# A graph and mixture-of-experts layer on one core: the last expert's rows scattered by slot, the second bias moved ahead of the first expert

## The chip, the cores and the metric

The kernel runs on one core of a Trainium2 chip. The metric is device time in microseconds (us) of one execution; lower is better. A core has TensorE (PE), VectorE (DVE), ScalarE (ACT), GpSimd (POOL) and SyncE (SP), each with its own instruction stream, and 16 DMA engines that all of them share. Semaphores order the streams.

## What is computed

The input is 625 rows of 768 numbers and 10,000 edges. After a two-layer graph convolution and an attention block, the part that matters here is a feed-forward layer with eight experts. Each row chooses one expert by the largest gate logit:

```python
w, sel = jax.lax.top_k(gate_logits, K)          # K = 1
w = jax.nn.softmax(w, axis=-1)
combine = jnp.zeros((n, E)).at[jnp.arange(n)[:, None], sel].add(w)
hid = jax.nn.relu(jnp.einsum('nd,edf->enf', h2, W1) + b1[:, None, :])
y = jnp.einsum('enf,efd->end', hid, W2) + b2[:, None, :]
moe = jnp.einsum('ne,end->nd', combine, y)
return x + moe.reshape(b, t, d)
```

W1 is 8 x 768 x 3072, W2 is 8 x 3072 x 768. So a result row is `base` (everything else that is added up) plus the row's weight times (its expert's y plus that expert's bias b2).

## The kernel before

**Rows, slots and chunks.** Rows are held as 5 groups (c = 0 to 4) of 125 on the partitions. Each expert has 128 slots. The routing gives each row a slot, `own` = 128 times its expert plus its rank there; `home` is the same unless an expert has more than 128 rows, when the surplus goes to extra tiles that run only if they are needed (in this profile they don't: the page shows 128 weight loads, 16 for each of 8 experts). GpSimd scatters the normalised rows `n2` by slot into DRAM (`hs_d`, L548) and later reads one expert's tile at a time back (`next_in`, L554). The first expert's tile is not waited for: TensorE makes it with products of one-hot marks `oh0` and `n2` (L1639).

**One expert.** An expert is 16 chunks of 1152 KB: 8 of W1, 8 of W2. SyncE loads a chunk into one of four `raw` buffers (L442, L445), ScalarE makes its high part `whi` (`split_hi`, L599), VectorE its low part `wlo` (`split_lo`, L894), which frees the raw buffer for the load four chunks later. TensorE multiplies three pairs of high and low parts: 18 products for a W1 chunk (L1675) and 18 for a W2 chunk (L1694). Between them the hidden tile is read (`hid`), turned (L1662), biased (`bia`, L1258) and split (`hTT`). The result y of an expert is in banks 4 and 5 of PSUM; for experts 0 to 6 it is read into `ysb` and stored by slot into `ys_d` (`y_out`, L559). `tile(0)` is written out for the first expert with a few things of its own; the other seven run in hardware loops on each engine.

**The end.** While the last expert runs, GpSimd gathers for each row its y from `ys_d` into `x2` (`y_back`, L563, five indirect DMAs); rows of the last expert get zeros. VectorE adds `wtok` times that to `base` (L1279). The last expert's y doesn't go through DRAM: ScalarE and VectorE split it, and TensorE spreads it back to the rows with products by turned marks `oh7T` (`spread_y`, L1715), on top of products of b2 with the turned choice `oh8T` (`bias_y`, L1710). VectorE adds `wtok` times the sum to `base` for each group (L1289), and SyncE stores the group (L456, two DMAs each).

**What sets the order.** Each engine's order is written out by hand. Around the change it is:

- TensorE ahead of the first expert: ranks (L1619, L1622), 50 filling products of a matrix of ones (`keep_busy`, L1330, whose results nobody reads), the first tile (L1639), 24 more filling products, then the first expert. In `tile(0)`, after chunk 1, `marks_turned` turns the marks of the last expert (L1648) and the choices (L1650). Its second half waits until ScalarE has copied both (`oh8T`, `oh7T`).
- ScalarE: splits of chunks 0 to 2, the first tile's scaling `hgf` (L819) and high part `hgh`, split of chunk 3, then `tile(0)`.
- VectorE: `hgl` (L894), the marks of the last expert (L1238), split of chunk 3, then `tile(0)`.
- GpSimd: a loop over experts 1 to 7 of `next_in` and `y_out`, then the five gathers, which wait until 10 of the last expert's 16 chunks are used (`Y_BACK_AT`).

## Time and profile before

| | us |
|---|---|
| three runs | 924.76 median, 922.78 to 930.63 |
| the profiled execution | 930.92 |
| its span | 929.40 (mean granted TensorE clock 0.971 of full) |
| PE busy | 874.0 (94%) |
| DVE busy | 705.7 (76%) |
| ACT busy | 556.4 (60%) |
| POOL busy | 90.3 (10%) |

The span runs from the first to the last instruction of the profiled execution; 1.52 us of its time lie outside it. Times in the rows count from the span's start. A matmul's duration overlaps with the next one's, so what 18 of them take is read from the chain of waits or from their starts. PEclk is the granted TensorE clock, 1.00 for 2.4 GHz and 0.50 for 1.2 GHz. In a timeline, brackets hold the engine's idle time before the row and what ended it; "issue" is time in which nothing that the profile shows was waited for.

### The profile page before, as it was taken

Reading aid. Unit: us, or ns where it says so; the run is one execution under the profiler, and the core shown is the slowest. Engines: PE = TensorE matmul, PEld = TensorE weight load, DVE = VectorE, ACT = ScalarE, POOL = GpSimd, SP = SyncE. Lnnn points to the kernel's source line nnn. Section 1 sums busy time; section 2 is a strip of 40 time slices with the busy share of each in tenths; the row PEclk is TensorE's granted clock in tenths of the full one; section 3 lists DMA queues with packets and bytes.
Section 4 is the critical chain, followed back from the end, with each engine's and each line's share of the span. In section 5 each row is a group of like instructions: output and inputs, shape, how many; then the busy total and the mean of one; then the engine's idle time right before and its main releaser. Section 6 shows DMA issues by size and latency. Waiting matters only on the chain.

```text
span 929.4 us, 14804 instructions
## 1 busy us (share of the span) xinstructions
PE 874.0 (94%) x5460; PEld 842.0 (91%) x5460; DVE 705.7 (76%) x1060; ACT 556.4 (60%) x780; POOL 90.3 (10%) x88
## 2 busy tenths in 40 slices
PE   7999898989998888899889999999999999999998
PEld 7899897989998667689889989999999999999996
DVE  7997155784333899855559889898998989898895
ACT  5503223154323788842548778787887878787870
POOL 2000006031000400012050000000000000000041
PEclk9999788999999999999799999999999999999998
DMA  7020006348114910060189999999999999999984
GB/s 228 3 101 1 1 2 119 85 101 183 55 51 112 326 71 2 1 185 1 36 254 327 331 349 354 376 335 377 363 361 377 354 378 344 379 358 368 369 288 130
DMA packets 116008, 196.01 MB, mean 211 GB/s; under 512 B 33828, under 2 KB 83196, under 8 KB 115958
## 3 DMA queue, kind: packets, MB, share of 16 engines
q1 hardware_dynamic: 107796, 169.08, 54.7%
q0 software_dynamic: 6336, 24.19, 7.8%
q10 hardware_dynamic: 1826, 2.06, 0.8%
q8 instruction: 33, 0.54, 0.2%
q14 instruction: 17, 0.14, 0.0%
HBM read 177.40 MB, written 17.90 MB: 210 GB/s over the span
## 4 chain that ended last, share of the span: by engine, by line
PE 43%; DVE 29%; DMA 13%; issue 7%; ACT 7%; SPq 0%; DVEq 0%; ACTq 0%
DVE wlo L894 14%; PE ps L1323 13%; DMA raw<-in_L_ffn_W 12%; PE ps L1499 7%; PE ps L1675 5%; PE ps L1694 5%; ACT whi L599 3%; DVE pr L1094 2%; DVE hTT L892 2%; DVE pTl L894 2%; PE ps L1352 1%; PE ps L1559 1%; DVE pr L1101 1%; DVE ohs L945 1%; DMA xs<-in_x 1%
## 5 line engine op out<-in xcount | busy, mean ns | idle before, releaser
L894 DVE TENSOR_TENSOR wlo<-raw,whi 128x2304 fp32r<-128x2304 f32 x137 | 350.9, 2570 | 23.7 <-ACT whi L599 23.5
L599 ACT ACTIVATE whi<-raw 128x2304 fp32r<-128x2304 f32 x139 | 296.2, 2132 | 83.4 <-DMA raw<-in_L_ffn_W 34.3
L1694 PE MATMUL ps<-whi,hTT 128*128 128x384 f32 x768 | 201.6, 339 | 1.0 <-ACT oh7T L599 1.0
L1694 PEld LDWEIGHTS ps<-whi,hTT 128*128 128x128 f32 x768 | 139.2, 188 | 1.2 <-ACT oh7T L599 1.2
L1675 PE MATMUL ps<-whi,hgh 128*128 128x384 f32 x384 | 134.1, 349 | 2.8 <-DVE hgl L894 2.8
L1675 PE MATMUL ps<-whi,hgl 128*128 128x384 f32 x384 | 130.3, 339 | 0.0
L1675 PE MATMUL ps<-wlo,hgh 128*128 128x384 f32 x384 | 129.8, 338 | 0.0
L1694 PE MATMUL ps<-wlo,hTT 128*128 128x384 f32 x384 | 129.0, 336 | 0.0
L1675 PEld LDWEIGHTS ps<-whi,hgh 128*128 128x128 f32 x384 | 73.3, 191 | 2.9 <-DVE hgl L894 2.9
L1675 PEld LDWEIGHTS ps<-wlo,hgh 128*128 128x128 f32 x384 | 73.2, 191 | 0.0
L1675 PEld LDWEIGHTS ps<-whi,hgl 128*128 128x128 f32 x384 | 73.0, 190 | 0.0
L1694 PEld LDWEIGHTS ps<-wlo,hTT 128*128 128x128 f32 x384 | 72.3, 188 | 0.0
L1352 PE MATMUL ps<-ohd,ohs 125*125 125x314 bf16 x400 | 58.2, 304 | 7.7 <-DVE ohd L946 5.7
L1352 PEld LDWEIGHTS ps<-ohd,ohs 125*125 125x125 bf16 x400 | 53.8, 139 | 10.9 <-DVE ohd L946 9.0
L1258 DVE TENSOR_TENSOR bia<-ps,b1T 128x384 f32<-128x384 f32 x64 | 35.6, 556 | 16.2 <-PE ps L1662 16.2
L606 ACT ACTIVATE root<-var 125x2 f32<-125x2 f32 (+2 forms) x13 | 2.7, 204 | 67.0 <-DVE var L914 66.9
L894 DVE TENSOR_TENSOR ql<-ps,qh 64x125 fp32r<-64x125 f32 (+1 forms) x66 | 21.8, 331 | 26.5 <-ACT qh L599 25.4
L1536 PE MATMUL ps<-ident,pr 125*125 125x125 f32 x168 | 30.6, 300 | 12.1 <-DVE pr L1101 7.6
L1536 PEld LDWEIGHTS ps<-ident,pr 125*125 125x125 f32 x168 | 22.4, 189 | 20.5 <-DVE pr L1101 9.5
L892 DVE SCALAR_TENSOR_TENSOR hTT<-bia,hTT 128x384 fp32r<-128x384 f32 x64 | 35.5, 554 | 5.6 <-ACT hTT L599 5.6
L599 ACT ACTIVATE qh<-ps 64x125 fp32r<-64x125 f32 (+1 forms) x66 | 20.1, 305 | 31.9 <-PE ps L1499 23.0
L756 ACT ACTIVATE pr<-pr,negmax 125x126 f32<-125x126 f32 (+4 forms) x60 | 36.0, 600 | 2.2 <-DVE negmax L1094 1.5
(282 smaller groups left out, 1761.6 us busy)
## 6 DMA issues: line engine op xcount, KB each, us to landing
raw<-in_L_ffn_W SPq DMA_DIRECT2D x128, 1152.0 KB, 6.9
hs_d<-bc POOLq DMA_DIRECT2D x13, 384.0 KB, 6.3
raw<-in_L_gnn_W SPq DMA_DIRECT2D x4, 1152.0 KB, 6.4
hs<-hs_d POOLq DMA_DIRECT2D x8, 384.0 KB, 5.6
ys_d<-ysb POOLq DMA_DIRECT2D x7, 384.0 KB, 6.0
raw<-in_L_ffn_Wv SPq DMA_DIRECT2D x6, 384.0 KB, 5.8
raw<-in_L_ffn_Wq SPq DMA_DIRECT2D x6, 384.0 KB, 5.2
raw<-in_L_ffn_Wk SPq DMA_DIRECT2D x6, 384.0 KB, 6.0
```

The source lines that it names most:

```text
L599: act.activation(out_, in_, func).then_inc(s, 1)
L756: act.activation(pr[:, u % PRS, 0:n], pr[:, u % PRS, 0:n], ACT.Exp, bias=negmax[:, u % 4, :], scale=-1.0, accum_out=ssum[:, u // 2 % 2, u ...
L892: dve.scalar_tensor_tensor(out_, in_, 0.0, hi_, ALU.max, ALU.subtract).then_inc(s, 1)
L894: dve.tensor_tensor(out_, in_, hi_, ALU.subtract).then_inc(s, 1)
L1094: dve.tensor_tensor_reduce(pr[:, u % PRS, 0:n], score_rows(u)[:, 0:n], cmask[:, (C - 1 - c) * P:(C - 1 - c) * P + n], -(float(D) ** -0.5), ...
L1258: dve.tensor_tensor(bia[:, k % 2, :, :], blocks(2 + k % 2, 128, JW, CAP), bcol.rearrange("p (j o) -> p j o", o=1).broadcast_to((128, JW, C ...
L1323: ins = mm(ps[0:P, bank + half, 0:HB], l, rr, start=m == 0 and i == 0, stop=m == DC - 1 and i == 2)
L1352: ins = mm(ps[0:P, m, 0:HALF], ohs[:, i % EU, m * P:(m + 1) * P], ohd[:, i % EU, :], start=i in BOUNDS, stop=i + 1 in BOUNDS)
L1499: ins = mm(ps[:, 2 * (m % 2) + half, 0:HALF], l, rr, start=c == 0 and i == 0, stop=c == DC - 1 and i == 2)
L1536: ins = nc.tensor.transpose(turned_part(u)[:, b, :], pr[:, u % PRS, b * P:(b + 1) * P], ident[0:P, 0:P])
L1675: ins = mm(ps[0:CAP, k % 2, 0:FW], l, rr, start=m == 0 and j == 0, stop=m == DC - 1 and j == 2)
L1694: ins = mm(ps[0:CAP, 4 + half, 0:HB], l, rr, start=k == 0 and j == 0 and jj == 0, stop=k == FCH - 1 and j == JW - 1 and jj == 2)
```

## The change

The last expert's rows are no longer spread back to the rows' order. They stay in slot order to the end: the part of `base` that belongs to them is scattered beforehand by slot into a DRAM buffer `bs_d` and read back as a 128 x 768 tile, the last y times a weight in slot order is added to it straight from PSUM (two VectorE instructions, L1352 of the new file), and one indirect DMA scatters the 128 rows to their places in the output (L606). The output as a whole is stored before that, group by group, as soon as the other experts' y is added; the scatter waits until these stores have landed, and writes the last expert's rows over. Row numbers and weights in slot order come from five small products in `tile(0)` (`last_rows`). The marks for this are made from `home` instead of `own`. The products for b2 are moved ahead of the first expert, where they take the place of the 74 filling products: groups 0 and 1 before the first tile is made, groups 4, 2 and 3 after it. ScalarE weighs them into `x2`, and VectorE adds them to `base` in the second half of the first expert. The gathers of the other experts' y wait for 4 used chunks of the last expert instead of 10. `b2h`, `b2l` and `oh8T` get a place of their own.

```diff
 AHEAD = 3
-LAST_BANK = (0, 2, 6, 4, 0)
-Y_BACK_AT = 10
+BIAS_BANK = (0, 4, 2, 4, 0)
+BIAS_FIRST, BIAS_THEN = (0, 1), (4, 2, 3)
+BIAS_STEPS = {FCH + 1: 0, FCH + 2: 1, FCH + 3: 2, FCH + 4: 3, FCH + 6: 4}
+Y_BACK_AT = 4
+FAR = 4096
...
-                sp.wait_ge(s_fin, c + 1)
+                sp.wait_ge(s_yin, c + 1)
                 for r0, r1 in PARTS:
                     sp.dma_start(tok(out)[r0:r1, c, :], base[r0:r1, c, :]).then_inc(s_out, 16)
...
-            with g.Fori(1, E) as t:
+            with g.Fori(1, E - 1) as t:
                 next_in(t)
                 y_out(t)
-            g.wait_ge(s_base, C)
+            g.wait_ge(s_slot7, 1)
+            for c in range(C):
+                g.wait_ge(s_b2a, c + 1)
+                g.indirect_dma_start(out=bs_d[:, :], out_offset=bass.IndirectOffsetOnAxis(ap=slot7[:, c:c + 1], axis=0),
+                                     in_=base[:, c, :], in_offset=None, bounds_check=CAP - 1, oob_is_err=False
+                                     ).then_inc(s_b7sc, 16)
+            g.wait_ge(s_b7sc, 16 * C)
+            g.dma_start(bc[0][0:CAP, :], bs_d[:, :]).then_inc(s_b7, 16)
+            next_in(E - 1)
+            y_out(E - 1)
             g.wait_ge(s_route, 1)
             g.wait_ge(s_yst, 16 * E)
             g.wait_ge(s_used, SCH * (E - 1) + Y_BACK_AT)
...
                 y_back(c, slot1)
             for c in range(C):
                 g.wait_ge(s_yg[c], 16)
+            g.wait_ge(s_row7, 1)
+            g.wait_ge(s_out, 32 * C)
+            g.wait_ge(s_y7, 2)
+            g.indirect_dma_start(out=out[:, :], out_offset=bass.IndirectOffsetOnAxis(ap=row7[:, 0:1], axis=0),
+                                 in_=ysb[0:CAP, :], in_offset=None, bounds_check=N - 1, oob_is_err=False
+                                 ).then_inc(s_out7, 16)
...
             for c in range(C):
+                if c == C - 1:
+                    a.wait_ge(s_b2in, 16)
+                    hi(b2h[:, :], bc[1][0:E, :], s_b2h)
                 root_of()
...
             split_hi(1, 0)
+            a.wait_ge(s_ohT, 1)
+            hi(oh8T[:, :, 0:P], blocks(4, E, C, P), s_ohl)
             split_hi(2, 0)
+
+            def bias_out(n, c):
+
+                a.wait_ge(s_b2y, n + 1)
+                act.activation(halves(x2[:, c, :]), wide(BIAS_BANK[c], P), ACT.Copy, scale=wtok[:, c:c + 1]
+                               ).then_inc(s_b2e, 1)
+
+            a.wait_ge(s_base, C)
+            a.wait_ge(s_wtok, 1)
+            for n, c in enumerate(BIAS_FIRST):
+                bias_out(n, c)
 
             def tile_part(n_in, part):
...
             tile_hi(DC)
+            for n, c in enumerate(BIAS_THEN):
+                bias_out(n + len(BIAS_FIRST), c)
...
-                    if first and k - 2 == OVER_N2:
-                        a.wait_ge(s_ohT, 1)
-                        hi(oh8T[0:E, :, :], blocks(4, E, C, P), s_ohl)
-                        hi(oh7T[:, :, :], blocks(6, 128, C, P), s_ohl)
...
-            a.wait_ge(s_b2in, 16)
-            a.wait_ge(s_used, SCH * (E - 1) + FCH + 6)
-            hi(b2h, bc[1][0:E, :], s_b2h)
-            for half in range(2):
-                a.wait_ge(*((s_used, SCH * E) if half else (s_yhalf, E)))
-                hi(whi[0][0:CAP, half * HB:(half + 1) * HB], ps[0:CAP, 4 + half, 0:HB], s_yh)
...
             for c in range(C):
+                if c == C - 1:
+                    d.wait_ge(s_b2h, 1)
+                    lo(b2l[:, :], bc[1][0:E, :], b2h[:, :], s_b2l)
...
             split_lo(2, 0)
             tile_in(1)
             for c in range(C):
-                dve.tensor_scalar(oh0[:, c, :], iotac[:, :], float(CAP * (E - 1)), own[:, c:c + 1],
+                dve.tensor_scalar(oh0[:, c, :], iotac[:, :], float(CAP * (E - 1)), home[:, c:c + 1],
                                   ALU.add, ALU.is_equal).then_inc(s_ohe, 1)
+            d.wait_ge(s_tokid, 1)
+            d.wait_ge(s_wtok, 1)
+            dve.tensor_copy(tokw[:, :, 0], tokid[:, :])
+            dve.tensor_copy(tokw[:, :, 1], wtok[:, :]).then_inc(s_tokw, 1)
+            before7, at7, far_at = (place[:, i, :] for i in range(3))
+            dve.tensor_scalar(before7, home, float(CAP * (E - 1)), None, ALU.is_lt)
+            step(dve.scalar_tensor_tensor(far_at, far, -float(FAR), tokid[:, :], ALU.mult, ALU.add))
+            step(dve.scalar_tensor_tensor(at7, before7, float(FAR), home, ALU.mult, ALU.add))
+            dve.tensor_scalar(farid[:, :], far_at, float(FAR - 1), None, ALU.add).then_inc(s_farid, 1)
+            dve.tensor_scalar(slot7[:, :], at7, -float(CAP * (E - 1)), None, ALU.add).then_inc(s_slot7, 1)
             split_lo(3, 0)
...
+                    if first and k == 4:
+                        d.wait_ge(s_row, 1)
+                        dve.tensor_copy(rowf[:, 0:2], ps[0:CAP, 6, 0:2]).then_inc(s_rowread, 1)
+                        d.wait_ge(s_rowread, 1)
+                        step(dve.tensor_scalar(rowf[:, 2:3], rowf[:, 0:1], 0.5, float(FAR), ALU.is_lt, ALU.mult))
+                        step(dve.scalar_tensor_tensor(rowf[:, 2:3], rowf[:, 0:1], -1.0, rowf[:, 2:3], ALU.add, ALU.add))
+                        dve.tensor_copy(row7[:, :], rowf[:, 2:3]).then_inc(s_row7, 1)
+                    if first and k in BIAS_STEPS:
+                        c = BIAS_STEPS[k]
+                        d.wait_ge(s_b2e, C)
+                        dve.tensor_tensor(base[:, c, :], base[:, c, :], x2[:, c, :], ALU.add).then_inc(s_b2a, 1)
...
-            d.wait_ge(s_b2h, 1)
-            lo(b2l, bc[1][0:E, :], b2h, s_b2l)
...
             for c in range(C):
                 d.wait_ge(s_yg[c], 16)
                 dve.scalar_tensor_tensor(base[:, c, :], x2[:, c, :], wtok[:, c:c + 1], base[:, c, :],
                                          ALU.mult, ALU.add).then_inc(s_yin, 1)
...
+            d.wait_ge(s_b7, 16)
+            d.wait_ge(s_yst, 16 * E)
             for half in range(2):
-                d.wait_ge(s_yh, half + 1)
+                d.wait_ge(*((s_used, SCH * E) if half else (s_yhalf, E)))
                 part = slice(half * HB, (half + 1) * HB)
-                lo(wlo[0][0:CAP, part], ps[0:CAP, 4 + half, 0:HB], whi[0][0:CAP, part], s_yl)
-            d.wait_ge(s_yin, C)
-            for c in range(C):
-                d.wait_ge(s_sel, c + 1)
-                bv = base[:, c, :].rearrange("p (a b) -> p a b", a=2)
-                dve.scalar_tensor_tensor(bv, wide(LAST_BANK[c], P), wtok[:, c:c + 1], bv,
-                                         ALU.mult, ALU.add).then_inc(s_fin, 1)
+                dve.scalar_tensor_tensor(ysb[0:CAP, part], ps[0:CAP, 4 + half, 0:HB], rowf[:, 1:2], bc[0][0:CAP, part],
+                                         ALU.mult, ALU.add).then_inc(s_y7, 1)
...
                 ins.then_inc(s_hgT, 1)
 
-            keep_busy(CHOICE_BUSY, onesb[:, :], onesb[:, :], 4)
+            pe.wait_ge(s_oh8, 2)
+            for c in range(C):
+                ins = nc.tensor.transpose(blocks(4, E, C, P)[:, c, :], rt[:, 3, c * E:(c + 1) * E], ident[0:P, 0:P])
+            ins.then_inc(s_ohT, 1)
+
+            def bias_y(c):
+
+                for half in range(2):
+                    for i, t in enumerate((b2h, b2l)):
+                        ins = mm(ps[0:P, BIAS_BANK[c] + half, 0:HB], oh8T[:, c, 0:P], t[:, half * HB:(half + 1) * HB],
+                                 start=i == 0, stop=i == 1)
+                ins.then_inc(s_b2y, 1)
+
+            pe.wait_ge(s_b2l, 1)
+            pe.wait_ge(s_ohl, 1)
+            for c in BIAS_FIRST:
+                bias_y(c)
             pe.wait_ge(s_oh0, C)
             for m in range(DC):
...
             ins.then_inc(s_hgT, 1)
-            keep_busy(TURN_BUSY, onesb[:, :], onesb[:, :], 3)
-
-            def marks_turned():
+            pe.wait_ge(s_b2e, len(BIAS_FIRST))
+            for c in BIAS_THEN:
+                bias_y(c)
+
+            def last_rows():
 
                 pe.wait_ge(s_ohe, C)
+                pe.wait_ge(s_tokw, 1)
                 for c in range(C):
-                    nc.tensor.transpose(blocks(6, 128, C, P)[:, c, :], oh0[:, c, :], ident[0:P, 0:P])
-                for c in range(C):
-                    ins = nc.tensor.transpose(blocks(4, E, C, P)[:, c, :], rt[:, 3, c * E:(c + 1) * E], ident[0:P, 0:P])
-                ins.then_inc(s_ohT, 1)
+                    ins = mm(ps[0:CAP, 6, 0:2], oh0[:, c, :], tokw[:, c, :], start=c == 0, stop=c == C - 1)
...
                 for k in range(FCH):
+                    if first and k < 2:
+                        pe.wait_ge(s_b2e, len(BIAS_FIRST) + 1 + 2 * k)
                     pe.wait_ge(s_mlo, SCH * t + k + 1)
...
                     if first and k == 1:
-                        marks_turned()
+                        last_rows()
                 if first:
-                    pe.wait_ge(s_ohl, 2)
+                    pe.wait_ge(s_rowread, 1)
...
-            pe.wait_ge(s_b2l, 1)
-            pe.wait_ge(s_hga, DC * (E + 1))
-            for c in range(3):
-                for half in range(2):
-                    bias_y(c, half)
-            pe.wait_ge(s_yl, 1)
-            for c in range(3):
-                spread_y(c, 0)
-            pe.wait_ge(s_yl, 2)
-            for c in range(3):
-                spread_y(c, 1).then_inc(s_sel, 1)
-            for c in range(3, C):
-                if c == C - 1:
-                    pe.wait_ge(s_fin, 1)
-                for half in range(2):
-                    bias_y(c, half)
-                    ins = spread_y(c, half)
-                ins.then_inc(s_sel, 1)
...
```

**TensorE, from the ranks to the first expert**, before and then after. `rt` holds the routing's small tables, `n2` the normalised rows, `whi2` and `hgh` a weight chunk and the first tile.

```order
L1622 MATMUL ps<-rt,onesb 125x8 x5
L1330 MATMUL ps<-onesb 125x125 x50
L1639 MATMUL ps<-oh0,n2 128x128 [waits first_tile_chosen]
L1639 MATMUL ps<-oh0,n2 128x128 x29
L1330 MATMUL ps<-onesb 125x125 x24
L1675 MATMUL ps<-whi2,hgh 128x384 [waits expert_lo,tile_lo]
```

```order
L1700 MATMUL ps<-ident,rt 8x125 [waits choice_made]
L1700 MATMUL ps<-ident,rt 8x125 x4
L1707 MATMUL ps<-b2h,oh8T 125x384 [waits experts_ready,b2_lo]
L1707 MATMUL ps<-b2l,oh8T 125x384
...
L1718 MATMUL ps<-oh0,n2 128x128 [waits first_tile_chosen]
L1718 MATMUL ps<-oh0,n2 128x128 x29
L1707 MATMUL ps<-b2h,oh8T 125x384 [waits bias_weighed]
L1707 MATMUL ps<-b2l,oh8T 125x384
...
L1757 MATMUL ps<-whi2,hgh 128x384 [waits expert_lo,bias_weighed,tile_lo]
```

The 50 filling products give way to five turns and 8 bias products (the pair stands four times), the 24 to 12 bias products (six times the pair), and the first expert waits for ScalarE's reading of group 4 as well.

**VectorE, second half of the first expert**, before and then after.

```order
L892 SCALAR_TENSOR_TENSOR hTT<-bia,hTT 128x384 [waits hidT_hi]
L894 TENSOR_TENSOR wlo2<-raw0,whi2 128x2304 [waits expert_hi]
L894 TENSOR_TENSOR wlo3<-raw1,whi3 128x2304 [waits expert_hi]
L894 TENSOR_TENSOR wlo0<-raw2,whi0 128x2304 [waits expert_hi]
L894 TENSOR_TENSOR wlo1<-raw3,whi1 128x2304 [waits expert_hi]
L894 TENSOR_TENSOR hgl<-hgf,hgh 128x768 [waits tile_hi]
```

```order
L937 SCALAR_TENSOR_TENSOR hTT<-bia,hTT 128x384 [waits hidT_hi]
L1336 TENSOR_TENSOR base<-base,x2 125x768 [waits bias_weighed]
L939 TENSOR_TENSOR wlo2<-raw0,whi2 128x2304 [waits expert_hi]
L1336 TENSOR_TENSOR base<-base,x2 125x768 [waits bias_weighed]
L939 TENSOR_TENSOR wlo3<-raw1,whi3 128x2304 [waits expert_hi]
L1336 TENSOR_TENSOR base<-base,x2 125x768 [waits bias_weighed]
L939 TENSOR_TENSOR wlo0<-raw2,whi0 128x2304 [waits expert_hi]
L1336 TENSOR_TENSOR base<-base,x2 125x768 [waits bias_weighed]
L939 TENSOR_TENSOR wlo1<-raw3,whi1 128x2304 [waits expert_hi]
L939 TENSOR_TENSOR hgl<-hgf,hgh 128x768 [waits tile_hi]
L1336 TENSOR_TENSOR base<-base,x2 125x768 [waits bias_weighed]
```

Five additions now stand between and behind the splits.

**GpSimd, from the expert loop's last store to the end**, before and then after. Names in brackets are semaphores.

```order
L559 DMA ys_d<-ysb 128x768
L569 REGISTER_ALU
L569 COMPARE_AND_BRANCH
L563 DMA x2<-ys_d,slot1 125x768 [waits y_stored,chunks_used,routed,base_made]
L563 DMA x2<-ys_d,slot1 125x768 x4
```

```order
L589 DMA bs_d<-base,slot7 128x768 [waits bias_added,last_slots_known]
L589 DMA bs_d<-base,slot7 128x768 [waits bias_added] x4
L593 DMA bc0<-bs_d 128x768 [waits last_base_sent]
L568 DMA hs<-hs_d 128x768 [waits tile_turned]
L573 DMA ys_d<-ysb 128x768 [waits y_read]
L577 DMA x2<-ys_d,slot1 125x768 [waits chunks_used,y_stored,routed]
L577 DMA x2<-ys_d,slot1 125x768 x4
L606 DMA out_x<-ysb,row7 625x768 [waits y_back4,last_rows_known,y_back3,out_stored,y_back2,last_out_made,y_back1,y_back0]
```

The loop ends one expert earlier; five scatters and one load stand between expert 6's store and the last expert's `next_in`, and the scatter to the output is the last DMA.

## Rows read from the trace of the kernel before

**Rows 1.** Window: length; busy PE, PEld, DVE, ACT, POOL; PEclk, DMA share, GB/s.
```profile
745.00:799.00 54.00, 53.67 (x320) 53.08 (x319) 49.24 (x35) 43.66 (x41) 1.08 (x2) 1.00 1.03 364
```
**Rows 2.** Chain of waits, last 35 us: start, duration, what.
```profile
895.22 18.72 PE ps L1694 x108
913.95 2.30 PE ps L1710 x12
916.25 3.45 PE ps L1715 x12
...
924.82 1.02 DVE base L1289
```
**Rows 3.** Timeline of VectorE and of SyncE's queue, last 20 us.
```profile
906.14 0.95 DVE L894 TENSOR_TENSOR hgl<-hgf,hgh 128x768 fp32r<-128x768 f32 x1
...
914.20 1.02 DVE L1279 SCALAR_TENSOR_TENSOR base<-x,wtok,base 125x768 f32<-125x768 f32 x1 [0.71 <-DMA x<-ys_d,slot]
```
```profile
919.57 8.00 SPq L456 DMA_DIRECT2D out_x<-base  x10
```
**Rows 4.** Windows of the tail, columns as in rows 1.
```profile
917.00:920.40 3.40, 3.40 (x11) 2.68 (x9) 1.88 (x3) 0.00 (x0) 0.00 (x0) 0.50 0.00 0
920.40:923.80 3.40, 3.40 (x14) 1.76 (x13) 2.01 (x3) 0.00 (x0) 0.00 (x0) 1.00 0.90 276
```
```profile
925.84:929.40 3.56, 0.00 (x0) 0.00 (x0) 0.00 (x0) 0.00 (x0) 0.00 (x0) 0.50 0.41 118
```
**Rows 5.** GpSimd's timeline, then the gathers' time from issue to landing.
```profile
465.10 6.15 POOL L548 DMA_INDIRECT hs_d<-n,slot  x1 [17.48 <-DVE slot L1217]
...
842.11 0.54 POOL L554 DMA_DIRECT2D hs<-hs_d  x1 [33.97 <-PE ps L1631]
...
907.61 1.20 POOL L563 DMA_INDIRECT x<-ys_d,slot  x1 [0.31 <-issue]
```
```profile
DMA to landing us min/median/max: 6.6/7.9/8.5
```
**Rows 6.** TensorE's timeline ahead of the first expert.
```profile
459.68 4.63 PE L1330 MATMUL ps<-onesb 125*125 125x125 bf16 x50
464.14 6.92 PE L1639 MATMUL ps<-oh,n 125*128 125x128 f32 x60
...
475.22 0.44 PE L1675 MATMUL ps<-whi,hgh 128*128 128x384 f32 x1 [2.76 <-DVE hgl L894]
```
**Rows 7.** Windows around the first expert's start, columns as in rows 1.
```profile
452.90:463.00 10.10, 10.10 (x86) 10.10 (x87) 7.25 (x39) 7.17 (x5) 0.00 (x0) 0.50 0.15 15
...
476.70:480.10 3.40, 3.40 (x13) 3.40 (x12) 2.08 (x1) 0.00 (x0) 3.13 (x1) 0.50 0.92 259
```
**Rows 8.** Groups by line and form: mean ns of one after the busy time.
```profile
L646 ACT ACTIVATE h<-ps 125x768 f32<-125x768 f32 x5 | 4.1, 811 | 25.5 <-PE ps L1323 25.5
```
```profile
L894 DVE TENSOR_TENSOR h1l<-tmp,h1h 125x768 fp32r<-125x768 f32 x5 | 4.8, 959 | 4.6 <-ACT h1h L599 4.6
```
**Rows 9.** First expert: ScalarE's and VectorE's timelines, and a piece of the chain of waits.
```profile
457.40 4.12 ACT L599 ACTIVATE whi<-raw 128x2304 fp32r<-128x2304 f32 x2
```
```profile
525.10 2.56 DVE L894 TENSOR_TENSOR wlo<-raw,whi 128x2304 fp32r<-128x2304 f32 x1 [3.13 <-ACT whi L599]
```
```profile
505.87 0.67 ACT oh7T L599
```
**Rows 10.** The weight stream: windows, landing of the W2 loads (L445), one chunk's splits.
```profile
874.00:888.00 14.00, 14.00 (x87) 13.87 (x86) 14.00 (x14) 11.88 (x13) 0.00 (x0) 1.00 1.00 356
808.00:823.00 15.00, 14.70 (x89) 14.31 (x88) 13.13 (x10) 12.11 (x12) 0.14 (x1) 1.00 1.05 374
```
```profile
DMA to landing us min/median/max: 5.3/5.5/6.8
```
```profile
885.16 2.55 DVE L894 TENSOR_TENSOR wlo<-raw,whi 128x2304 fp32r<-128x2304 f32 x1
```
```profile
898.46 2.13 ACT L599 ACTIVATE whi<-raw 128x2304 fp32r<-128x2304 f32 x1 [1.03 <-PE ps L1694]
```

More of the change, by code:

```diff
@@ L146, in build @@
         slot2 = sb("slot2", [P, C], I32)
+        slot7 = sb("slot7", [P, C], I32)
+        farid = sb("farid", [P, C], I32)
+        tokid = sb("tokid", [P, C], F32)
+        tokw = sb("tokw", [P, C, 2], F32)
+        place = sb("place", [P, 3, C], F32)
+        rowf = sb("rowf", [CAP, 3], F32)
+        row7 = sb("row7", [CAP, 1], I32)
         over = sb("over", [1, 1 + K_OVER], I32)
@@ L190, in build @@
                     [("n2", [P, C, D], F32), ("h2T", [128, DC, NP], F32)],
[L191 to L192 removed]
+                    [("r3pad", [128, RB - 2 * DF // 128 * CAP], F32),
                      ("hTT", [128, FCH, 2, JW, CAP], F32R)])
@@ L460, in _ @@
                     weights(e, s + E)
-                sp.wait_ge(s_out, 32 * C)
-                for c in range(C):
-                    sp.wait_ge(s_fin2, c + 1)
-                    for r0, r1 in PARTS:
-                        sp.dma_start(tok(out)[r0:r1, c, :], base[r0:r1, c, :]).then_inc(s_out2, 16)
-                sp.wait_ge(s_out2, 32 * C)
+                sp.wait_ge(s_out2, 16 * C)
             sp.wait_ge(s_out, 32 * C)
+            sp.wait_ge(s_out7, 16)
         @block.gpsimd
```

56 lines of the change are left out of this document (31 added, 25 removed).

## The prediction

> **What bounds the kernel now.** I read the windows first, expert by expert. The reader is to see an engine and a transport that are both full: in the window of one expert's length TensorE is busy 53.67 of 54 us and the DMA engines' share is 1.03 [rows 1]. So the eight experts can hardly be shortened by small edits, and anything that holds up TensorE or the weight stream there is paid. Second comes the chain of waits from its end: the last expert product ends at 913.95 (895.22 + 18.72, with rounding), and 15.45 us of span follow it [rows 2]: products of b2 (2.30), products that spread y (3.45 and more), the additions behind them, the last one ending at 925.84, and 3.56 us in which no engine works and the stores land [rows 2, 4]. TensorE's clock falls to 1.2 GHz at 917.0 for 3.4 us, right after the twelve products of b2, although TensorE had not stopped [rows 4]. Third, the timelines of VectorE and GpSimd in the tail and ahead of the first expert: these hold the durations of what is added.
>
> **The tail: what goes and what is late next.** All of TensorE's and ScalarE's work behind the last product goes. What remains are two threads, and the scatter waits for both.
> Thread one, y: ScalarE and TensorE have no part; the second half of y is a 128 x 384 addition from PSUM, half as wide as the 1.02 us one [rows 3], so 0.5 us: 914.5.
> Thread two, the stores of the whole output: VectorE is free at 907.1 after `hgl` [rows 3] and the gathers have long landed, so five additions of 1.0 us end at 912.1. The first store is issued at 908.1; in the trace the first was issued at 919.57 and the DMA engines are at work from 920.4 on [rows 3, 4], so data move from 909.0. They are 1.92 MB (625 x 768 x 4 bytes), at the 276 GB/s of the window behind 920.4 [rows 4] 7.0 us: 916.0. The other bound, last addition to end of span as now (3.56 us, [rows 4]), gives 915.7. I take 916.0. So y is not the late one: the scatter waits for stores of rows that are mostly not its own, some 1.5 us.
> Then the scatter: GpSimd starts 0.3 us after what frees it, as between the gathers [rows 5], at 916.3. The trace has no such scatter into a quiet DMA system. The nearest row is the gather of the same size: 6.6 us from issue to landing at best, median 7.9, at most 8.5 [rows 5]; the last one was issued at 907.61 in 1.20 us, and VectorE waited for it until 914.20 [rows 3, 5]. VectorE is idle when the scatter is issued, so I take the best, 6.6: landed at 922.9, and 0.3 for the last wait: 923.2 instead of 929.4, a gain of 6.2. With 8.5 it is 4.3; if it lands like SyncE's plain stores (3.56 to the end) the end is 919.9, a gain of 9.5.
> The issue itself has a trap: the first indirect DMA of the trace took 6.15 us at 465.10 beside two long VectorE splits, and the last, with VectorE hardly at work, 1.20 [rows 5]. The Trainium skill (SBUF — State Buffer, section SBUF: two separate sides) says that GpSimd can't write descriptors while a VectorE instruction holds the port that they share; the trace agrees, and by that rule the last scatter, with VectorE at rest, is safe, while the moved gathers and the five new scatters issue slowly, which nobody waits for.
>
> **Ahead of the first expert.** Now 50 filling products run from 459.68, the clock is at 1.2 GHz from 452.9 until 463.0, and the first tile's products start at 464.14 and take 6.8 us, 0.113 each at 2.4 GHz, without a gap ahead of them [rows 6, 7]. After: five turns of 0.2 us from 459.7; ScalarE, done with its first split at 459.5 (457.40 and half of 4.12, [rows 9]), copies `oh8T` in 0.67 as it did `oh7T` [rows 9], to 461.5; then 8 bias products. At 2.4 GHz twelve took 2.30 us [rows 2], 0.19 each; at half the clock I take somewhat less than double, 0.33: 2.6 us, to 464.1. So the start of the first tile is where it was, but with less dense work ahead of it. I let the clock rise 2.3 us into the tile's products: ten of 60 at 0.226 instead of 0.113 cost 1.1 us. Bounds: the clock rises at 463.0 as before and the bias products end early, -0.4; it stays low for all 60, +6.8.
> Behind the tile, 12 bias products take 2.3 us where the gap to the first expert is 4.2 (471.0 to 475.22, [rows 6]): hidden. ScalarE's reading of a group, 0.81 us [rows 8], stands behind `hgh` and beside VectorE's `hgl`; the first expert needs one of them at its start and three at its second chunk, 3 x 0.81 = 2.4 us after `hgh`, with a chunk of over 3 us between: hidden, 0.1 at worst. The readings of groups 0 and 1 fall in ScalarE's idle time. Split 3 comes 2.4 us later on ScalarE and the load behind it too; its buffer is not wanted until three chunks later. The b2 split, under 1 us on each of two engines, moves to where both engines wait for the projection. Front: +1.1.
>
> **In the first expert.** Removed: TensorE waited for ScalarE's copies, `oh7T` among them, 0.67 each, at 505 to 506.6 [rows 9]. The wait that replaces it is long over. But the stretch behind is bound by the weight stream, so not all of the 1.2 us comes back: I take -0.7 (bounds 0 and -1.2). The ten turns after chunk 1 give way to ten small products (five in two passes): 0. Added on VectorE: four tiny instructions, and five additions of 0.96 us [rows 8], 4.8 us, between the splits that free the raw buffers. VectorE waits 3.13 us at 525.10 [rows 9], ahead of the fourth split behind the additions, which swallows what the first four have piled up; until then several loads are in flight. I take +0.3, bounds 0 and +2.
>
> **The stream in experts 6 and 7.** Five scatters of `base` and the load back put at most 0.8 MB (2 x 393 kB) on the queues behind 808, at share 1.05 and 374 GB/s [rows 10]: 2.1 us if all of it displaced weights. Most of it moves later, when slack is back, and rows out of bounds move nothing: +0.4. GpSimd has the 33.97 us for it that it now waits until 842.11 [rows 5], so `next_in` isn't late. The gathers, 1.92 MB, move from 895 to 874: 5.4 us at 356 GB/s [rows 10]. There a raw buffer is free at 887.7 (885.16 + 2.55) and wanted at 898.46, 10.8 us, and its load lands after 5.5 [rows 10]: 5.2 us of slack per buffer, and the gathers come 2.8 us apart. I take +0.2, bounds 0 and +5.4.
>
> **Sum.** -6.2 + 1.1 - 0.7 + 0.3 + 0.4 + 0.2 = -4.9 us. The profiled execution took 930.92 (span 929.40), so it would become 926.0. It is slower than the median of the three runs, 924.76; I apply the difference to the median: 919.9 us.
>
> **Rivals.**
> B, the scatter is quick: it lands like a plain store, gain 9.5 in the tail, in all -8.2: 916.6 us. For it: every row is one piece of 3 KB and nothing else is on the queues. Against: none of the five gathers came under 6.6. The Trainium skill (DMA: Bandwidth & Descriptors, section Anatomy of one DMA) fits 2.0 us plus bytes at 436 GB/s for a DMA issued by GpSimd, an estimate of 2.9 us here; by it the gain would be larger still, but the trace's gathers of the same bytes took more than twice that. Chance 0.15.
> C, the slower one: the clock. The filling products are gone, and in the tail the clock fell after the very products that replace them. If it stays at 1.2 GHz through the first tile (+6.8 in place of +1.1) and the first expert runs a second stretch like that of 476.7 to 480.1 (3.4 us at half, 1.7 lost, [rows 7]), the sum is -4.9 + 5.7 + 1.7 = +2.5: 927.3 us. It decides once the first expert starts more than 6 us late. Against: the tile's own products are dense, and dense work brought the clock back each time. Chance 0.08.
> D, the stream pays in full: 2.1 + 5.4 in place of 0.6 is +6.9, in all +2.0: 926.8 us. Against: the slack per buffer. Chance 0.10.
> E, the change doesn't shorten the tail: the wait for the stores and the landing (8.5) eat most of it, gain 3, in all -1.7: 923.1. Chance 0.12.
> The forecast itself: 0.55.
>
> **How the numbers follow.** The likeliest case gives 919.9, its own range 917 to 923. B and E widen it to 915 at the low end and beyond 923; C and D reach 927, of which the range takes in most: 915.0 to 927.0. A measurement of this kernel tells about 1% (9.2 us) from no change. Faster by more than that means under 915.5: the far part of B, with some noise, 0.13. Slower by more than that, over 934.0, needs C and D together: 0.04. Within 1%: 0.83.
>
> **What would show each step.** In the profile after: no matmul behind the last expert product; its end to the end of span near 9.3 us (15.45 now). The scatter's issue row with about 1.2 us, starting 2 us after the last product, with the stores and not VectorE as its releaser. The first tile's 60 products in 7 to 9 us and the first expert's start near 476.3. Five additions of 1.0 us between VectorE's splits, and no larger TensorE waits at experts 1, 6 and 7. The prediction is wrong if the scatter lands in under 4 us, if the stores are in before y, if the first tile takes over 10 us, or if TensorE waits over 1 us for weights behind 808.

## The result and the profile after

| | before | after |
|---|---|---|
| median of the timed runs, us | 926.00 (4 runs, 922.78 to 930.63) | 944.23 (4 runs, 941.51 to 947.49) |
| ratio | 1 | 1.0177, 95% interval 1.0140 to 1.0214 |
| profiled execution (span), us | 930.92 (929.4) | 947.49 (945.6) |

The change makes the kernel slower by 1.8%, 16.2 us between the two profiled spans. The forecast was 919.9 us.

First, the windows of the last expert, of the kernel after. Columns as in [rows 1]: length; busy PE, PEld, DVE, ACT, POOL; PEclk, DMA share, GB/s.

```profile
855.00:880.00 25.00, 24.96 (x146) 24.61 (x145) 20.91 (x13) 19.97 (x17) 0.54 (x1) 1.00 1.06 376
880.00:894.00 14.00, 14.00 (x87) 13.78 (x85) 14.00 (x13) 8.96 (x10) 11.35 (x5) 1.00 1.00 305
894.00:898.00 4.00, 0.50 (x3) 0.27 (x2) 0.27 (x1) 2.82 (x3) 1.36 (x1) 0.88 1.03 257
898.00:903.00 5.00, 4.68 (x21) 4.36 (x20) 3.58 (x3) 0.09 (x1) 0.00 (x0) 0.76 1.05 268
903.00:906.00 3.00, 0.29 (x3) 0.30 (x4) 0.00 (x0) 2.85 (x3) 0.00 (x0) 1.00 1.03 246
```

From 881 on GpSimd issues the five gathers. TensorE, which had been busy 38.96 of the 39 us up to 894, stands nearly still in two windows of 4 and 3 us, and its clock is granted only in part between them. The DMA engines stay full, share 1.00 to 1.05, and yet move 246 to 305 GB/s where they moved 376. In [rows 10] the same part of the last expert ran at 356 without the gathers. What TensorE waits for stands on ScalarE's timeline, whose splits feed it:

```profile
895.18 2.12 ACT L636 ACTIVATE whi<-raw 128x2304 fp32r<-128x2304 f32 x1 [4.90 <-DMA raw<-in_L_ffn_W]
903.15 2.12 ACT L636 ACTIVATE whi<-raw 128x2304 fp32r<-128x2304 f32 x1 [5.06 <-DMA raw<-in_L_ffn_W]
910.26 2.13 ACT L636 ACTIVATE whi<-raw 128x2304 fp32r<-128x2304 f32 x1 [4.20 <-DMA raw<-in_L_ffn_W]
```

Three splits wait 4 to 5 us for weights. The weight loads issued from 870 on take a median of 12.3 us from issue to landing, where [rows 10] had 5.5:

```profile
DMA to landing us min/median/max: 6.6/12.3/19.3
```

The gathers' own time from issue to landing, the answer to [rows 5], has doubled:

```profile
DMA to landing us min/median/max: 9.9/15.7/18.1
```

Second, the tail: VectorE's additions and SyncE's stores, GpSimd's scatter, and the last instructions of the sequencers (q behind the engine's name; duration min/median/max in ns, then the start).

```profile
924.40 4.73 DVE L1345 SCALAR_TENSOR_TENSOR base<-x,wtok,base 125x768 f32<-125x768 f32 x5
```
```profile
925.44 5.93 SPq L471 DMA_DIRECT2D out_x<-base  x10
```
```profile
937.07 1.03 POOL L606 DMA_INDIRECT out_x<-ysb,row  x1 [41.71 <-issue]
```
```profile
L478 SPq EVENT_SEMAPHORE  x1: 17/17/17, 940.1 to 940.1; - x1
```
```profile
L88 DVEq DRAIN  x1: 17/17/17, 930.6 to 930.6; - x1
L88 PEldq DRAIN  x1: 73/73/73, 931.6 to 931.6; - x1
L88 POOLq DRAIN  x1: 5134/5134/5134, 940.2 to 940.2; - x1
L88 SPq DRAIN  x1: 7/7/7, 940.3 to 940.3; - x1
L88 SPq EVENT_SEMAPHORE  x1: 17/17/17, 945.5 to 945.5; - x1
```

The last product ends at 929.08. The stores are in at 936.05 (930.96 + 5.09, the last DMA piece of the chain of waits, below), the scatter's issue begins 1.0 later, SyncE sees it landed at 940.1, and then 5.5 us pass in which nothing moves. DRAIN is the instruction that stands at the end of each engine's program. Every engine has drained by then but GpSimd, whose DRAIN takes 5.13 us; all others end when it does. That is 7.0 + 1.0 + 3.0 + 5.5 = 16.5 us where 15.45 stood [rows 2].

```profile
930.96 5.09 DMA out_x<-base
```

The view of waits is misleading here. It names TensorE's sequencer, which had drained at 931.6:

```profile
SPq L88 <- PEq L88: 5.3, 1, 5.3
```

The chain ends with the scatter and doesn't show the drain. It stands at the line of the last instructions. In the kernel before the same instruction is there, but begins as soon as the gathers have landed, beside ten microseconds of TensorE's work:

```profile
L85 POOLq DRAIN  x1: 4481/4481/4481, 915.3 to 915.3; - x1
L85 SPq DRAIN  x1: 13/13/13, 929.2 to 929.2; - x1
```

Third, ahead of the first expert, TensorE's timeline of after, against [rows 6]:

```profile
463.95 0.52 PE L1707 MATMUL ps<-b2l,oh8T 8*125 8x384 f32 x1
464.40 9.80 PE L1718 MATMUL ps<-oh,n 125*128 125x128 f32 x60
474.13 0.44 PE L1707 MATMUL ps<-b2h,oh8T 8*125 8x384 f32 x1
...
478.36 0.69 PE L1757 MATMUL ps<-whi,hgh 128*128 128x384 f32 x1 [1.86 <-DVE hgl L939]
```

The bias products run at 1.2 GHz (0.32 apart), the first tile takes 9.80 us (6.92), and the first expert starts at 478.36 (475.22). It starts at low clock and stays there for 5.6 us, where before it spent 3.4 us at low clock after 1.5 at full [rows 7], so its first chunk ends later by another microsecond. This second stretch is not the same in every execution. At the same place the kernel before, and below it the same code up to here with only the gathers moved (the second run of the next section), had:

```profile
477.36 0.52 PE L1675 MATMUL ps<-wlo,hgh 128*128 128x384 f32 x1
```
```profile
477.32 0.33 PE L1675 MATMUL ps<-wlo,hgh 128*128 128x384 f32 x1
```

So that runs can be compared stretch by stretch, I read four landmarks in every profile: the start of the first tile's products, GpSimd's issues of the stores of the first and of the last-but-one expert's y (stores 1 and 7 of seven), the last product, and the end. All differences, us:

| kernel | tile to first expert | tile to y store 1 | tile to y store 7 | y store 7 to last product | last product to end |
|---|---|---|---|---|---|
| before | 11.1 | 71.3 | 397.3 | 52.5 | 15.4 |
| after | 14.0 | 74.1 | 403.5 | 61.2 | 16.5 |

The start of the tile is within 0.3. The loss is +6.2, then +8.7, then +1.1. Each is the difference of two single profiles, and no timed run of either kernel was slower than its profile. The runs below give the spread: up to y store 7 three profiles of the code of before took 392.8 to 397.3 (mean 394.4), six of the code of after 398.0 to 403.5 (400.9), so the early loss of 6.2 is about the mean one, 6.5. With the gathers at 4, the stretch behind took 61.2 to 66.9 in six profiles, and 8.7 stands at the low end.

### The profile page after: what moved, and what is told of

Its sections match the earlier page's. It is cut to its first block, busy times and chain, and to the rows that moved or that the text cites. A ratio compares the mean times of both kernels' runs of the same rounds, so it can differ in the third digit from the quotient of the medians.

```text
span 945.6 us, 14652 instructions
## 1 busy us (share of the span) xinstructions
PE 870.6 (92%) x5371; PEld 839.2 (89%) x5371; DVE 707.3 (75%) x1071; ACT 559.2 (59%) x782; POOL 98.7 (10%) x97
## 3 DMA queue, kind: packets, MB, share of 16 engines
q1 hardware_dynamic: 107796, 169.08, 53.9%
## 4 chain that ended last, share of the span: by engine, by line
PE 37%; DVE 33%; DMA 14%; issue 8%; ACT 7%; SPq 0%; DVEq 0%; POOL 0%; POOLq 0%; ACTq 0%
DVE wlo L939 16%; DMA raw<-in_L_ffn_W 12%; PE ps L1386 12%; PE ps L1562 7%; PE ps L1757 4%; PE ps L1776 3%; ACT whi L636 2%; DVE hTT L937 2%; DVE pr L1139 2%; PE ps L1622 2%; DVE pTl L939 2%; PE ps L1415 1%; DVE bia L1316 1%; DVE ohs L990 1%; DMA xs<-in_x 1%
## 5 line engine op out<-in xcount | busy, mean ns | idle before, releaser
L1776 PE MATMUL ps<-whi,hTT 128*128 128x384 f32 x768 | 203.7, 341 | 0.0
L1415 PEld LDWEIGHTS ps<-ohd,ohs 125*125 125x125 bf16 x400 | 54.0, 140 | 11.1 <-DVE ohd L991 9.2
L937 DVE SCALAR_TENSOR_TENSOR hTT<-bia,hTT 128x384 fp32r<-128x384 f32 x64 | 35.4, 552 | 16.1 <-ACT hTT L636 16.0
L1742 PE MATMUL ps<-ident,hid 128*128 128x128 f32 x192 | 32.6, 279 | 12.0 <-ACT hid L905 12.0
L1742 PEld LDWEIGHTS ps<-ident,hid 128*128 128x128 f32 x192 | 24.2, 142 | 17.6 <-ACT hid L905 15.8
```

Of the source, the lines that this page charges most:

```text
L937: dve.scalar_tensor_tensor(out_, in_, 0.0, hi_, ALU.max, ALU.subtract).then_inc(s, 1)
L1415: ins = mm(ps[0:P, m, 0:HALF], ohs[:, i % EU, m * P:(m + 1) * P], ohd[:, i % EU, :], start=i in BOUNDS, stop=i + 1 in BOUNDS)
L1742: ins = nc.tensor.transpose(blocks(2 + k % 2, 128, JW, CAP)[:, j, :], hid[0:CAP, k % 2, j * 128:(j + 1) * 128], ident[0:CAP, 0:CAP])
L1776: ins = mm(ps[0:CAP, 4 + half, 0:HB], l, rr, start=k == 0 and j == 0 and jj == 0, stop=k == FCH - 1 and j == JW - 1 and jj == 2)
```

## The experiments

Times are medians; ratios are to the kernel before on the same chip, with their 95% intervals. The columns of the table above follow for all runs behind the last experiment.

### Gathers late again, and gathers early in the kernel before

```diff
-Y_BACK_AT = 4
+Y_BACK_AT = 10
```


> The changed kernel, but the five gathers of the earlier experts' outputs are issued once ten of the last expert's twelve weight chunks are used, as before the change, and no longer at four. Theory: the gathers beside the last expert's weight stream stall TensorE and are worth +8.7 us of the changed kernel's excess, so it falls from 944.2 to about 935.5, no gap of TensorE over 1 us stands near 894 to 906, and the clock stays up there; the gathers' late landing may give back up to 2 us in the tail. Rival: the stall comes from the stream being late from the start or from the load of the last bases, and the gathers only stand beside it: the time stays within 2 us of 944 and the gaps remain.

(The chunks of an expert are miscounted as twelve here; there are sixteen.) Measured: 935.46, 1.0085 (1.0057 to 1.0112), 9 us less than after. The second run is the same edit the other way round, in the kernel before (10 to 4):

> The kernel before, with only the gathers moved from ten used chunks of the last expert to four. Theory: the gathers alone stall the last expert, 926.0 + 8.7 = about 934.7 us, with loads of W2 landing in over 15 us in place of 5.3. Rival (it takes the scatters into the small tensor, the later stream or the software queue's work before it as well): within 2 us of 926.

Measured: 936.85, 1.0088 (1.0059 to 1.0117), +9.5. From y store 7 to the last product 64.1 us instead of 52.5. The two together show that the moved gathers alone cost 8 to 9 us. That it is the place of these gathers is shown; what in them costs it (the queue, the rows taken by address, or any bytes beside the weights) is not, since no run puts a plain load there. The five scatters into `bs_d`, which the first of these kernels still has, cost little: from y store 6 to y store 7 it takes 54.3, before 53.9.

### Filling products with few rows

```diff
-            keep_busy(CHOICE_BUSY, onesb[:, :], onesb[:, :], 4)
+            keep_busy(CHOICE_BUSY, onesb[0:E, :], onesb[0:E, :], 4)
```


> The kernel before, with the 50 filling products ahead of the first tile reading 8 partitions of their operands in place of 128: as many instructions of the same kind with as many columns. Theory: products with few rows do not bring TensorE's clock back though the engine is busy, so the clock is still at 1.2 GHz when the first tile's products start at 464.1; these take about 9.8 us in place of 6.8, the first expert starts about 3 us later, and the time is 926.0 + 3 to 6, 929 to 932. Rival: only the engine's busy time counts, the clock rises at 463.0 as before, 926.0 within 1 us.

Measured: 928.98, 1.0020 (1.0002 to 1.0038). Of this run, the filling products and the tile, and two windows:

```profile
460.48 5.59 PE L1330 MATMUL ps<-onesb 8*125 8x125 bf16 x50
```
```profile
466.00 9.78 PE L1639 MATMUL ps<-oh,n 125*128 125x128 f32 x60
```
```profile
463.60:466.00 2.40, 2.40 (x24) 2.28 (x23) 2.09 (x16) 0.00 (x0) 0.17 (x1) 0.50 1.05 388
466.00:471.00 5.00, 5.00 (x24) 5.00 (x24) 4.83 (x2) 0.00 (x0) 5.00 (x1) 0.50 0.26 57
```

The same 50 products, as long and as dense, but with 8 rows of operands in place of 125, leave the clock at 1.2 GHz to the end and for 5 us of the tile; with 125 rows it was up from 463.0 on [rows 7]. The tile took 9.78 us, as after. The mechanism is as expected; the whole price, 1.9 us, is below what I expected (3 to 6). Part of that may be another stretch: in this profile the first expert ran at full clock throughout, where [rows 7] had 3.4 us at half.

### The overflow count read ahead of the scatter

```diff
+            n_over = g.value_load(over[0:1, 0:1], min_val=0, max_val=K_OVER)
             g.wait_ge(s_row7, 1)
```


> The changed kernel, with GpSimd's read of the overflow count into a register moved from behind the last scatter to ahead of it, where GpSimd waits for the stores. Theory: the 5.5 us between the last scattered row and the end of the span are the scatter's own completion on its queue, which nothing on the engine shortens: 944.2 within 1 us. Rival: they are the read and the branch behind the scatter: about 940 or less, and the end of the span comes within 1.5 us of the last data.

Measured: 945.17, 1.0194 (1.0165 to 1.0224): no gain. So the emptiness isn't the read and the branch. My other reading, the scatter's completion, was wrong as well, as the next four runs show.

### A plain store in place of the scatter, by GpSimd and by SyncE

```diff
-            g.indirect_dma_start(out=out[:, :], out_offset=bass.IndirectOffsetOnAxis(ap=row7[:, 0:1], axis=0),
-                                 in_=ysb[0:CAP, :], in_offset=None, bounds_check=N - 1, oob_is_err=False
-                                 ).then_inc(s_out7, 16)
+            g.dma_start(out[0:CAP, :], ysb[0:CAP, :]).then_inc(s_out7, 16)
```


> The changed kernel, whose last scatter (an indirect store of 128 rows at addresses from a table, issued by GpSimd) gives way to a plain store of the same 128 rows to fixed rows, issued by GpSimd at the same place, with the same waits. The output's rows then stand in the wrong place. In the changed kernel 8.5 us pass from the scatter's issue to the end, 5.5 of them behind its last data. Theory A: this is the completion of any DMA that GpSimd issues, so nothing changes: 8 to 9 us from issue to end, 944.7 within 1.5. Theory B: it belongs to the indirect form, and the plain store ends 2 to 3 us after its issue: about 939.

> The same plain store of 128 rows to fixed rows, issued by SyncE in place of GpSimd's scatter, with the same waits for the stores and for y. Theory A (the completion of a DMA that GpSimd issues is what is long): about 5 us less than the changed kernel, 939 to 940, and about 3 us from issue to end. Rival C (any DMA that is issued alone at the end has this long completion): 944.7 within 1.5 and over 7 us from issue to end.

Measured: 944.06, 1.0160 (1.0123 to 1.0197), and 945.73, 1.0192 (1.0162 to 1.0222). From the store's issue to the end it is 8.2 and 9.3 us, with the scatter 8.5. By this and by the times neither form nor queue matters, which seemed to bear out that any lone DMA at the end completes slowly. The sequencers' last line says otherwise. This is the run with SyncE's store, issued at 934.19 and landed by 938.3:

```profile
L88 POOLq DRAIN  x1: 5052/5052/5052, 938.3 to 938.3; - x1
```

GpSimd still waited for the store there, so its drain still began only then.

### GpSimd's drain exposed in before, and taken away in after

```diff
+            g.wait_ge(s_out, 32 * C)
```
at the end of GpSimd's program in the kernel before:

> The kernel before, with one line more: GpSimd too waits for all stores of the output before it ends. The records of the changed kernel show GpSimd's DRAIN at the end of the program taking 5.13 us from 940.2, and every other engine's end waiting for it; in the kernel before it takes 4.48 us from 915.3, beside TensorE's last products. Theory (the drain is a fixed price of GpSimd's end, paid wherever its last wait ends): it starts at 929.2 and the span ends about 5.1 us later, 931 to 933 for a median of 926 to 927.9 before. Rival (the drain is long only because an indirect or software DMA has just run, in the changed kernel): within 1 us of before.

Measured: 930.80, 1.0059 (1.0034 to 1.0085), +3.7 by the medians. In the profile the drain runs from 922.2 for 4.48 us and the last product is followed by 19.3 us in place of 15.4:

```profile
L85 POOLq DRAIN  x1: 4481/4481/4481, 922.2 to 922.2; - x1
L85 SPq DRAIN  x1: 13/13/13, 922.2 to 922.2; - x1
```

One line, a wait that SyncE has as well, costs four microseconds. The other way round, SyncE's plain store with GpSimd's last wait taken out:

> The kernel of the plain store issued by SyncE in place of the scatter (945.7, ratio 1.0192), in which GpSimd no longer waits for that store. Theory: GpSimd's drain of 5 us then lies beside the last product and the stores, the span ends at 0.3 us after the plain store has landed, some 4 us after its issue, and the time falls by 5 us: 940 to 941. Rival: the 5 us are the store's completion: 945 to 946.

Measured: 936.61, 1.0074 (1.0047 to 1.0101). The drain lies at 911.5, SyncE's store is issued at 932.30 and the span ends at 935.0, 2.7 us later where it was 9.3. The gain by the medians, 9, is more than the 5 expected. The two profiles, 8.5 us apart, say where it lies: 3.8 in the tail (9.4 in place of 13.2), which the edit touches; 3.2 up to y store 7, 1.0 from there to the last product and 0.6 ahead of the tile, which it doesn't. In those stretches profiles of the same code differ by as much, so only the 3.8 goes to the drain.

### Additions of the bias

```diff
-                        dve.tensor_tensor(base[:, c, :], base[:, c, :], x2[:, c, :], ALU.add).then_inc(s_b2a, 1)
```


> The changed kernel with late gathers (935.5, ratio 1.0085 to before) and without VectorE's five additions of the weighed bias to the base in the first expert; the scatters of the base wait for ScalarE's readings instead. It leaves out the second bias. Theory: the additions stand between the splits that free the raw buffers, the weight stream is late by 1 to 2 us after them for good, so the time falls to 933.5 to 934.5. Rival: VectorE's slack hides them, 935.5 within 0.7, and the whole early lag is that of the clock ahead of the first expert.

Measured: 933.66, 1.0067 (1.0038 to 1.0096). By the medians -1.8, which the intervals don't tell from nothing. In the profile tile to y store 7 is 395.8, where six kernels with the additions show 398.0 to 403.5; but it is the profile of this kernel's fastest execution, 3.0 us under its median.

### Full-row filling products ahead of the bias products

```diff
+            keep_busy(30, onesb[:, :], onesb[:, :], 7)
             pe.wait_ge(s_b2l, 1)
```


> The changed kernel with late gathers (935.5, ratio 1.0085 to before), with 30 filling products of 128 rows put between the five turns of the marks and the first eight bias products, where TensorE otherwise waits 0.9 us. Theory: dense products of full rows bring the clock back before the first tile, whose 60 products then take about 7 us in place of 9.8; the fillers themselves delay its start by 1 us at most, so the first expert starts about 2 us sooner and its first chunk runs at full clock: 932 to 933.5. Rival: the bias products, with 8 rows, drop the clock again or the fillers' own time eats the gain: 935 to 937.

Measured: 936.63, 1.0098 (1.0074 to 1.0123): the rival's number. The clock does come back, the bias products are 0.17 apart and the tile takes 6.96 us; but thirty products take 3.41 us where 0.9 was idle, so they put the tile off by some 2.5 us. (It starts at 467.76, but without them it starts anywhere from 460.44 to 467.24 in the other kernels of after.) Whether the eight bias products fail to raise the clock in the kernel after because of their few rows, or because they are few, no run separates; the run with 8-row filling products shows that few rows alone can do it.

### The edits together

GpSimd reads the count first and doesn't wait for the scatter's landing; three of the five additions stand behind VectorE's fourth split, and the gathers are late.

> The changed kernel with late gathers (935.5, ratio 1.0085 to before) and two edits: GpSimd reads the overflow count ahead of the last scatter and does not wait for its landing (SyncE does), so that its drain starts 2.1 us sooner; and three of VectorE's five bias additions stand ahead of its first product of the first expert, in an idle stretch of 3.5 us. Theory: -2 for the drain, -1 for the additions, 932.0 to 933.5. Rival: drain waits for the queue's own completion whenever it starts, and the additions cost nothing where they were: 935 to 936.

Measured: 932.36, 1.0058 (1.0035 to 1.0081). The drain now begins right at the scatter's issue, 3.3 us ahead of its landing, and takes 1.1 us longer; from the scatter's issue to the end it is 6.5 us in place of 8.5:

```profile
L88 POOLq DRAIN  x1: 6234/6234/6234, 924.1 to 924.1; - x1
```

> As the previous one, with the gathers issued at eight used chunks of the last expert's sixteen in place of ten. At ten they land last, and VectorE's last addition waits for them until 3 us after the last product, with the stores behind it; at four they hold up the weight stream. Theory: at eight, two more weight loads (of 1.2 MB, about 3.4 us each) are still to be issued and get the gathers beside them: the stall of TensorE is 2 to 4 us, the gathers are in by the last product: a net of -1 to +2, 932 to 935. Rival: the stall of nine us comes whenever any load is behind the gathers: 937 to 941.

Measured: 934.39, 1.0066 (1.0037 to 1.0095). Two late loads with gathers beside them cost 1.7 us of the stretch (55.8 against 54.2), not 9, and the tail isn't shorter (15.0 against 14.9), since the stores' 5.5 us behind the last addition remain.

> The kernel before, with the first expert's fourth weight split, on ScalarE and on VectorE, moved ahead of the turned first tile, where ScalarE waits 9.6 us and VectorE 4.1 us. Its raw buffer is refilled some 7 us sooner. Theory: the stream is the bound from the first expert on, a sooner load is a lead that lasts, and the time falls by 1 to 3 us (ratio 0.997 to 0.999). Rival: the first expert's start and its first chunk's end set all later splits, a sooner fourth split changes nothing: ratio 1.000 within 0.001.

> The changed kernel with late gathers, GpSimd freed at the end and three additions early (932.4, ratio 1.0058), and the same move of the fourth split. Theory: the split stood 5 us late behind the readings of the bias products, so the move is worth 2 to 3 us: 929.5 to 930.5, ratio 1.003. Rival: as above it changes nothing and the lag is that of the clock alone: 932.4 within 1.

Measured: 926.88, 1.0013 (0.9985 to 1.0040), and 929.76, 1.0047 (1.0018 to 1.0075). The moved split is worth nothing that can be told in either kernel. The last has the lowest ratio of the versions with the scatter, though its interval overlaps those of the two before it, and it is still slower than before.

| kernel | to first expert | to y store 1 | to y store 7 | to last product | to end |
|---|---|---|---|---|---|
| before, gathers at 4 | 11.1 | 68.3 | 392.8 | 64.1 | 15.3 |
| before, GpSimd waits | 11.2 | 68.5 | 393.0 | 52.5 | 19.3 |
| before, split early | 11.1 | 70.0 | 395.3 | 52.5 | 14.6 |
| before, 8-row fillers | 13.9 | 70.5 | 395.4 | 52.6 | 14.9 |
| after, gathers at 10 | 14.0 | 74.1 | 402.1 | 54.2 | 17.3 |
| after, count first | 12.7 | 71.8 | 398.0 | 62.4 | 16.1 |
| after, GpSimd's plain store | 12.6 | 71.5 | 400.4 | 66.9 | 12.7 |
| after, SyncE's plain store | 12.8 | 71.8 | 402.4 | 65.1 | 13.2 |
| the same, GpSimd free | 13.7 | 73.4 | 399.2 | 64.1 | 9.4 |
| gathers at 10, no additions | 12.7 | 70.7 | 395.8 | 52.8 | 17.0 |
| gathers at 10, fillers first | 11.1 | 70.1 | 394.8 | 52.8 | 16.8 |
| together, gathers at 10 | 12.8 | 70.8 | 396.3 | 54.2 | 14.9 |
| together, gathers at 8 | 12.6 | 70.5 | 395.9 | 55.8 | 15.0 |
| together, split early | 12.7 | 70.6 | 397.7 | 54.2 | 14.1 |

## Why the prediction was wrong, step by step

- **"I take +0.2" for the gathers: this is the step that failed most.** Measured 8.7 in the profile, 9 and 9.5 by the two medians (8.5 and 8.2 by the ratios). The slack per buffer, 5.2 us, was set against a load's landing in a quiet stream, and the upper bound, 5.4, took the rate of 356 GB/s as given. But the rate itself fell to 246 to 305 with the engines still full, so the gathers cost more than their bytes. Three of the five took 15.7 us or more to land. Rival D had the right mechanism with a chance of 0.10, and even its full price was too small.
- **"The tail: a gain of 6.2."** From the last product to the end 9.3 was forecast, 16.5 measured, a loss of 1.1 against before. Its numbers failed one by one. The stores: 2.05 us behind the last product were forecast, 7.0 measured, because the additions begin 4.7 us ahead of the last product (924.40 to 929.08) and not 6.9, and the stores are in 6.9 us behind the last addition, not 3.9. SyncE's ten issues are part of that: they take 5.93 us, 1.2 for a group's two, and the additions only 0.95, so the last store is issued 1.8 us behind the last addition and lands 5.1 later. GpSimd: 0.3 until the scatter's issue was forecast, 1.0 measured; the issue itself took 1.03, so the trap named in the prediction did not spring. The landing: 6.6 was taken from the gathers, 3.0 was measured, as rival B said. The fit in the Trainium skill (DMA: Bandwidth & Descriptors, section Anatomy of one DMA) gives an estimate of 2.9 for 128 rows, and this trace agrees. And the end: 0.3 us for the last wait was forecast, 5.5 measured. This is GpSimd's drain, which no term held and which the trace of before showed in a row that the prediction didn't read. Without it the tail would be 11.0 us, 4.4 shorter than before.
- **"In the first expert: -0.7, +0.3" and "Front: +1.1".** Together +0.7 was forecast, about +6 measured by y store 7. The forecast let the clock rise 2.3 us into the tile's products. It rose 5 to 6 us into them, at 470; the tile took 9.8, in other kernels of the same code 8.5 to 9.8, and the first expert starts 1.5 to 3 us later, 2.2 on the mean of six. That is the mechanism of rival C, at less than half its size (+2.9 of the 6.8 that it allowed for). The additions, "+0.3", can be read from one more landmark, y store 2, counted from the first expert's start. Among the kernels of after whose clock in the first expert is alike (full, then 1.2 GHz, then full again by 6 us), four with all five additions between the splits took 114.5 to 116.1 us; four without them, or with three of them moved, took 112.8 to 113.0. So the additions cost about 2.2 us in the first two experts. In their stretch VectorE of after has no idle time at all between 514 and 537; before it waited 3.13 us there [rows 9]. What is left of the 6.5, some 2 us, stays open, the "-0.7" with it. The clock in the first expert has a part in it: of three profiles with the code of before, the two whose clock stayed up took 111.5 and 112.0 to y store 2, the third [rows 7] 115.9, as much as the slower kernels of after. By the medians (-1.8 for no additions, +1.2 for the fillers) none of this can be told, since they move by as much from one set of runs to the next.
- **"+0.4" for the scatters into the small tensor was right** as far as it can be told: from y store 6 to 7 it takes 54.0 us against 53.9 in the two profiles, 54.2 against 53.8 on the mean of the eleven kernels with the scatters and the five without, and `next_in` isn't late; GpSimd waits 16.70 us ahead of it.
- **"0.04" for slower by over 1%** rested on C and D coming together, each at the price given. C came at less than half its price, D at more than its full one, and the drain, which stood in no case, took back more than the rest of the tail gained.

The ledger of the profiles: +6.2 early, +8.7 gathers, +1.1 tail (of which the drain is +5.5 and the rest -4.4) make 16.0 of 16.2 us; the start of the tile holds 0.3. Of the prediction's own signs of being wrong two came, a landing under 4 us and TensorE waiting over 1 us for weights behind 808; none of them would have shown the drain.

## What to carry to other kernels

A transfer moved into a stretch where the DMA engines are full should be priced by what such a transfer does to the rate of all, and an edit of its place alone, in either kernel, is the cheapest test of it. When the last work of a kernel goes to an engine that used to be done early, look at that engine's last instructions in the trace of before: a fixed cost of ending may be hidden there. Products put in the place of filling products must be judged by whether the clock rises with them, in a row, and not by how densely they run.

## What the hardware showed that I had not expected

- GpSimd's DRAIN at the end of the program takes 4.48 us (before), 5.05 to 5.13 (after) and 6.23 to 6.24 when it begins at the issue of a scatter; ScalarE's takes 8 ns and SyncE's 7 to 13.
- Gathers beside a weight stream: 246 to 305 GB/s at a share of 1.00 to 1.05, where the stream alone moves 356 to 376.
- Fifty products with 8 rows of operands, 0.11 us apart without a gap, left the clock at 1.2 GHz, in the one profile of them; fifty with 125 rows brought it to 2.4 in all four.
- A scatter from 128 slots of 3 KB, 0.33 MB moved, into a quiet system landed 3.0 us after its issue, GpSimd's plain store of all 128 (0.39 MB) 2.7. The gathers of 125 such rows took 6.6 at best [rows 5], beside other transfers.
